# Sixteen full tiles of the expert lists worked beside the last group's scatters in a gated attention and mixture-of-experts block

## The chip, the core and the metric

The kernel runs on one core of a Trainium2 chip. The metric is the device time of one execution in microseconds (us), the median of several runs. The profile shows one further execution. Its span is the stretch from the first to the last instruction; what lies around the span is in the execution's own time.

## What is computed

The input is x of 16 x 128 x 256, a context tensor of the same shape, and weights. The reference, cut to what matters:

```python
# first half: x = x + tanh(g_xattn) * attention(ctx, ctx, layernorm(x))
kv_f = jnp.fft.rfft(einsum('bhil,bhjl->bijhl', k_, v_), n=2 * L)
y = jnp.fft.irfft(kv_f * kernel_f, n=2 * L)[..., :L]
out = einsum('bijhl,bhil->bjhl', y + kv * D, q_)
# second half: x = x + tanh(g_ffn) * ffn(layernorm(x)), for each of T = 2048 tokens
scores = sigmoid(xf @ w_router)                   # 32 experts
masked = where(best 4 of 8 groups, scores + corr_bias, -inf)
_, topk_idx = jax.lax.top_k(masked, 6)            # six experts for a token
eo = einsum('etm,emh->eth', silu(g) * u, down_w)  # 256 -> 176 -> 256 in each expert
routed = einsum('te,eth->th', combine, eo)
shared = silu(xf @ sh_gate_w) * (xf @ sh_up_w) @ sh_down_w
```

A token is one of 16 x 128 rows of 256 values. 2048 tokens with six experts each are 12288 rows of expert work.

## The kernel before

**Groups.** The sixteen batch rows go in four groups of GB = 4 (`group(g, ...)` on each engine; g runs from -1, which only makes the first attention, to 3, which only routes). In a group TensorE does the convolutions of the next group's attention, the router and the shared expert of this one; VectorE makes the attention sums and layernorms (L562 on), picks the experts (`choose`, L634) and finds each row's place in its expert's list (`place_rows`, L690). GpSimd (POOL) then writes the group's 4 x 128 tokens into the lists `expert_lists` in DRAM, with 24 indirect DMAs of 128 rows (L369). A row has 289 values: the normalised token, its number and its 32 scores. The rows wait in SBUF in one of two buffers `pay[g % 2]`; one lies in the arena, the other is `payload`.

**Weights.** The big SBUF region `arena` holds the attention's buffers first and the experts' weights `wgu` (gate and up) and `wd` (down, on 88 partitions) later. Thirteen experts' `wgu` is loaded early. The rest of `wgu` and the first 17 experts' `wd` are issued on ScalarE's DMA queue once the last attention is summed (L469, L471). `wd` of experts 17 to 24 lies over the scratch area and the arena's payload buffer, and is issued on ScalarE's queue after group 2's scatters and the tile tables (L500). `wd` of experts 25 to 31 is issued on SyncE's (SP's) queue after group 3's shared expert is added (L282).

**Tables.** After group 3's routing VectorE counts the rows of each expert (L783), cuts each list into tiles of 128 rows and makes a table with each tile's first row, expert and the rows that it has in common with the tile before (`describe_tiles`, `spread_tables`). PE spreads it over the partitions (L1021).

**Tiles.** Then all engines run through the tiles in blocks of four; 108 tiles run in this input. For tile t SP loads 128 rows of the list into `payload[:, t % 4]` (L289), PE transposes them (L1045), VectorE copies (L847), PE multiplies with `wgu` (L1054), ScalarE and VectorE make silu times up (L507, L865), PE transposes (L1064) and multiplies with `wd` (L1073), ScalarE scales by the token's score into a buffer (`copy_y`, L522; four buffers), and POOL adds the 128 rows to `token_sums` in DRAM with one indirect DMA (`add_tile`, L383), which waits for the add of three tiles before. SP's load of tile t waits until tile t - 3 has been picked from and transposed. Each engine works strictly in the order of its program; the semaphores named in the code are all that joins them.

**The turn from groups to tiles.** SP loads tile 0 only when `payload_free` has reached NG + 1, that is when all four groups' scatters have landed:

```python
            sp.wait_ge(payload_free, NG)
            sp.wait_ge(sh_added, GB)
            sp.dma_start(wd[:, WD_LAST * WD_E:E * WD_E], ...).then_inc(late_in, 16)
...
            sp.wait_ge(tables_ready, 1)
            sp.wait_ge(payload_free, NG + 1)
```

PE waits for all four weight transfers (`late_in` at 64) before its first tile. POOL issues group 3's scatters only after group 2's have landed, since it waits for a group's 24 before it goes on. At the end three partial sums are read back, added to x and stored.

## Time and profile before

| | us |
|---|---|
| median of 3 runs | 587.53 |
| lowest and highest | 586.39 and 587.93 |
| the profiled execution's own time | 592.33 |
| its span | 590.2 |
| TensorE busy in the span | 443.5 (75%) |
| VectorE, ScalarE, GpSimd busy | 313.5, 200.1, 301.0 |
| DMA traffic | 89.68 MB, mean 152 GB/s |

The profile has a page (busy times, the span in slices, the chain that ended last, the costliest groups of instructions) and views of single stretches: the chain of waits, the timeline, windows with each engine's busy time, and the DMA queues. Among the DMA queues q0 carries GpSimd's indirect transfers, q1 those that SP issues and q10 those that ScalarE issues. Times are counted from the start of the span.

### The profile page before, as it was taken

How to read it: one execution, taken by the hardware profiler on the slowest of the kernel's cores; microseconds unless marked ns; L12 is line 12 of the kernel's file. 1: busy time of each engine (PE TensorE's matmuls, PEld its weight loads, DVE VectorE, ACT ScalarE, POOL GpSimd, SP SyncE). 2: the span in 40 equal slices, each digit the busy share in tenths (PEclk: the TensorE clock that was granted, in tenths of full speed). 3: DMA queues.
4: the chain of work that ended last, by engine and by line, in shares of the span. 5: the costliest groups of instructions: out<-in, count | busy, mean ns of one | idle time of the engine just before them, and what ended most of it. 6: DMA issues, size and time to landing. Idle time of an engine off the chain costs nothing.

```text
span 590.2 us, 8581 instructions
## 1 busy us (share of the span) xinstructions
PE 443.5 (75%) x2098; PEld 334.7 (57%) x2098; DVE 313.5 (53%) x1141; ACT 200.1 (34%) x506; POOL 301.0 (51%) x240
## 2 busy tenths in 40 slices
PE   0181798789889666800599999999999999999700
PEld 0171676666767445500477777777777777777500
DVE  3679979966994804500344444444444444444227
ACT  2050633632553231100144444444444444444300
POOL 2800008865884760077066576666666666666610
PEclk9995889988969966955699999999999999999955
DMA  6999402221221498576356766666666666666488
GB/s 257 343 285 416 200 1 99 89 92 68 90 95 70 164 390 231 134 209 193 82 105 110 118 115 111 111 111 116 111 114 114 114 114 116 115 115 117 57 265 323
DMA packets 55706, 89.68 MB, mean 152 GB/s; under 512 B 6525, under 2 KB 49885, under 8 KB 55005
## 3 DMA queue, kind: packets, MB, share of 16 engines
q0 software_dynamic: 20160, 28.37, 28.4%
q1 hardware_dynamic: 35150, 49.33, 25.3%
q10 hardware_dynamic: 342, 11.35, 6.2%
q8 instruction: 23, 0.38, 0.3%
q14 instruction: 31, 0.25, 0.1%
HBM read 47.00 MB, written 42.03 MB: 151 GB/s over the span
## 4 chain that ended last, share of the span: by engine, by line
PE 67%; DVE 11%; issue 8%; DMA 5%; ACT 3%; POOL 2%; another core or an unknown queue 2%; SPq 1%; DVEq 0%; POOLq 0%; ACTq 0%
PE bank L1054 22%; PE bank L1073 15%; PE bank L943 6%; PE bank L914 4%; PE bank L1045 4%; PE bank L1064 4%; DVE arena L603 4%; PE bank L964 4%; PE bank L915 2%; DMA arena<-toeplitz 2%; PE bank L985 2%; DMA arena<-token_sums 2%; PE bank L934 2%; POOL work L354 1%
## 5 line engine op out<-in xcount | busy, mean ns | idle before, releaser
L383 POOL DMA_INDIRECT token_sums<-work,dest x108 | 168.3, 1558 | 113.8 <-ACT work L522 99.5
L1054 PE MATMUL bank<-wgu,work 128*128 x432 | 146.9, 463 | 0.0
L1073 PE MATMUL bank<-wd,work 88*128 x432 | 111.0, 379 | 0.0
L369 POOL DMA_INDIRECT expert_lists<-arena,slots x48 | 59.8, 1246 | 82.3 <-DVE slots L703 68.3
L865 DVE TENSOR_TENSOR work<-work,bank 128x176 f32<-128x176 f32 x108 | 36.4, 337 | 120.2 <-ACT work L507 120.2
L1054 PEld LDWEIGHTS bank<-wgu,work 128*128 128x128 f32 x432 | 74.1, 192 | 23.2 <-issue 0.5
L369 POOL DMA_INDIRECT expert_lists<-payload,slots x48 | 57.4, 1195 | 53.2 <-DMA expert_lists<-arena,slots 31.9
L507 ACT ACTIVATE work<-bank 128x176 f32<-128x176 f32 x108 | 34.2, 317 | 141.5 <-PE bank L1054 141.5
L847 DVE COPY work<-bank 128x256 f32<-128x256 f32 x108 | 45.8, 424 | 59.4 <-PE bank L1045 58.2
L1073 PEld LDWEIGHTS bank<-wd,work 88*128 88x128 f32 x432 | 73.3, 190 | 6.1 <-issue 0.2
L522 ACT ACTIVATE work<-bank,work 128x256 f32<-128x256 f32 x108 | 51.1, 473 | 53.6 <-issue 49.3
L1045 PE MATMUL bank<-ident,payload 128*128 128x128 f32 x216 | 42.2, 277 | 34.6 <-DMA payload<-expert_lists 34.6
L1045 PEld LDWEIGHTS bank<-ident,payload 128*128 128x128 f32 x216 | 30.8, 144 | 46.7 <-DMA payload<-expert_lists 35.8
L943 PE MATMUL bank<-shgu_sb,arena 128*128 128x352 f32 x128 | 49.1, 535 | 0.0
L914 PE MATMUL bank<-arena 128*128 128x288 f32 x128 | 44.0, 426 | 4.1 <-ACT arena L416 2.3
L603 DVE TENSOR_TENSOR arena<-arena,q_sb 128x448 f32<-128x448 f32 (+7 forms) x120 | 45.1, 451 | 2.2 <-ACT arena L416 2.2
L1064 PEld LDWEIGHTS bank<-ident,work 128*88 128x88 f32 x216 | 26.6, 123 | 29.9 <-issue 18.5
L1064 PE MATMUL bank<-ident,work 128*88 128x128 f32 x216 | 41.3, 273 | 0.0
L514 ACT COPY work<-bank 88x256 f32<-88x256 f32 x108 | 39.7, 367 | 0.0
L934 PE MATMUL bank<-ident,arena 128*128 128x128 f32 x48 | 9.8, 355 | 34.1 <-POOL arena L358 27.5
L943 PEld LDWEIGHTS bank<-shgu_sb,arena 128*128 128x128 f32 x128 | 27.7, 228 | 13.8 <-issue 6.2
L416 ACT COPY arena<-bank 128x288 f32<-128x288 f32 x64 | 25.3, 399 | 28.1 <-PE bank L915 27.0
(137 smaller groups left out, 506.8 us busy)
## 6 DMA issues: line engine op xcount, KB each, us to landing
payload<-expert_lists SPq DMA_DIRECT2D x108, 144.5 KB
wgu<-w_gu ACTq DMA_DIRECT2D x1, 6688.0 KB
arena<-token_sums SPq DMA_DIRECT2D x12, 512.0 KB, 8.3
expert_lists<-blank SPq DMA_DIRECT2D x1, 4768.5 KB, 26.7
wgu<-w_gu SPq DMA_DIRECT2D x1, 4576.0 KB, 17.5
token_sums<-blank SPq DMA_DIRECT2D x1, 4480.0 KB, 36.5
wd<-w_down ACTq DMA_DIRECT2D x1, 2992.0 KB
arena<-toeplitz SPq DMA_DIRECT2D x1, 2048.0 KB, 12.1
```

Source lines behind the costliest of these rows:

```text
L369: nc.gpsimd.indirect_dma_start(lists, bass.IndirectOffsetOnAxis(ap=slots[:, g % 2, b, k:k + 1], axis=0), pay[g % 2][:, b, :], None).then_i ...
L383: nc.gpsimd.indirect_dma_start(sums, bass.IndirectOffsetOnAxis(ap=dest[:, t % NPICK:t % NPICK + 1], axis=0), y_row(t), None, compute_op=AL ...
L514: nc.scalar.copy(win(work, HT_AT + t % 2 * L, [[1, L]], parts=MH), bank[4 + t % 2][0:MH, 0:L]).then_inc(t_hT_copied, 1)
L522: nc.scalar.activation(y_row(t), bank[6 + t % 2][:, 0:L], ACT.Identity, scale=pick_w(t)).then_inc(t_y_copied, 1)
L603: last = nc.vector.tensor_tensor(win(arena, Z_AT + z0, [[DH * DH, CELLS], [1, DH - d]]), y, win(q_sb, q_at + i0, [[DH, CELLS], [1, DH - d] ...
L847: nc.vector.tensor_copy(win(work, XT_AT + t % 2 * L, [[1, L]]), bank[t % 2][:, 0:L]).then_inc(t_x, 1)
L914: nc.tensor.matmul(y[:, 0:2 * CB], toe(h, 0), prods(s, hh, 0, 2), start=True, stop=False)
L943: last = nc.tensor.matmul(bank[5 + half][:, 0:SHM], x2T(b, k), shgu_sb[:, k, half * SHM:(half + 1) * SHM], start=(k == 0), stop=(k == KC - 1))
L1045: last = nc.tensor.transpose(bank[t % 2][:, k * P:(k + 1) * P], payload[:, t % NX, k * P:(k + 1) * P], ident[:, :])
L1054: last = nc.tensor.matmul(bank[2 + t % 2][:, 0:2 * M], xT_half(t, k), wgu[:, bass.ds(e * WGU_E + k * 2 * M, 2 * M)], start=(k == 0), stop= ...
L1064: last = nc.tensor.transpose(bank[4 + t % 2][0:MH, c * P:(c + 1) * P], win(work, H_AT + t % 2 * M + c * MH, [[1, MH]]), ident[:, :])
L1073: last = nc.tensor.matmul(bank[6 + t % 2][:, 0:L], hT_half(t, c), wd[:, bass.ds(e * WD_E + c * L, L)], start=(c == 0), stop=(c == 1))
```

## The change

Group 2's routing now also counts the rows that groups 0 to 2 have put in each list (twelve small matmuls and a copy to `count_a`). In group 3 VectorE makes a first table from it (`describe_known`), of the first NA = 16 tiles that are wholly filled, among the first 17 experts; PE spreads it and `spread_known` stores it. The later table leaves these tiles out (`taken_a`). SP loads tiles 0 to 3 when `payload_free` has reached NG (groups 0 to 2 have landed), then issues the last weights, then loads tiles 4 to 15, and only then waits for the second table and the last group's scatters. PE waits for two of the weight transfers before the first tile and for the other two at the gate matmuls of tile 16. Group payloads no longer lie in the arena, so the last two weight transfers are cut in another place: experts 17 to 21 on ScalarE's queue, 22 to 31 on SP's. Results wait in sixteen buffers, taken from arrays that are free by then, and `copy_y` of tile t waits for the add of tile t - 16.

The core of the diff:

```diff
-TMP_SIZE = 2912
+TMP_SIZE = 2432
...
-PAY_AT = TMP_AT + TMP_SIZE
-X2T_AT = PAY_AT + GB * ROW
+X2T_AT = TMP_AT + TMP_SIZE
...
-        pay = [win(arena, PAY_AT, [[ROW, GB], [1, ROW]]), payload[:, :, :]]
+        pay = [payload[:, :, :], payload_2[:, :, :]]
...
-            sp.wait_ge(payload_free, NG)
-            sp.wait_ge(sh_added, GB)
-            sp.dma_start(wd[:, WD_LAST * WD_E:E * WD_E], w_down[:, WD_LAST * WD_E:E * WD_E]).then_inc(late_in, 16)
-
...
+            sp.wait_ge(tables_a_ready, 1)
+            sp.wait_ge(payload_free, NG)
+            for t in range(NX):
+                load_tile(t)
+            sp.wait_ge(sh_added, GB)
+            sp.dma_start(wd[:, WD_LAST * WD_E:E * WD_E], w_down[:, WD_LAST * WD_E:E * WD_E]).then_inc(last_in, 16)
+            for t in range(NX, NA):
+                load_tile(t)
+
             sp.wait_ge(tables_ready, 1)
             sp.wait_ge(payload_free, NG + 1)
             last = last_block(sp)
-            for t in range(4 * (SURE + 1)):
+            for t in range(NA, 4 * (SURE + 1)):
                 load_tile(t)
...
             act.wait_ge(tables_ready, 1)
-            act.wait_ge(payload_free, NG)
             act.dma_start(wd[:, WD_MID * WD_E:WD_LAST * WD_E],
-                          w_down[:, WD_MID * WD_E:WD_LAST * WD_E]).then_inc(late_in, 16)
+                          w_down[:, WD_MID * WD_E:WD_LAST * WD_E]).then_inc(last_in, 16)
...
-                if t >= NX:
-                    act.wait_ge(t_added[t % NX], nth(t - NX))
+                if t >= YR:
+                    act.wait_ge(t_added[t % NX], nth(t - YR))
...
+                    if g == NG - 2:
+                        nc.vector.tensor_copy(count_a[:, :], bank[4][:, 2 * GB * E:(2 * GB + 1) * E])
...
+                    if not attend:
+                        describe_known(link)
...
+                    if not attend:
+                        spread_known()
+                    place_rows(*chosen)
...
+                chain(nc.vector.tensor_tensor(flat(nt, E), flat(nt, E), taken_a[:, :], ALU.subtract))
...
+                    else:
+                        pe.wait_ge(meta_a_ready, 1)
+                        for c in range(2):
+                            last = nc.tensor.matmul(bank[1][:, c * NA:(c + 1) * NA], win(arena, WIDE_A_AT + c * P, [[1, P]]),
+                                                    ident[:, 0:NA], start=True, stop=True)
+                        last.then_inc(meta_a_spread, 1)
...
+                    if g == NG - 2:
+
+                        for seen in range(KNOWN):
+                            last = nc.tensor.matmul(bank[4][:, 2 * GB * E:(2 * GB + 1) * E], ones_b[:, :],
+                                                    win(mask_b, seen * E, [[1, E]]), start=(seen == 0),
+                                                    stop=(seen == KNOWN - 1))
+                    last.then_inc(rank_ready, 1)
...
+                if t == NA:
+                    pe.wait_ge(last_in, 32)
...
-            pe.wait_ge(late_in, 64)
+            pe.wait_ge(late_in, 32)
```

SP's program at the turn from groups to tiles, before; `token_sums<-arena` are the stores of the shared expert of groups 0 to 2, `wd<-w_down` is L282:

```order
L272 DMA token_sums<-arena 128x256 [waits sh_stored,sh_copied] x11
L282 DMA wd<-w_down 88x3584 [waits sh_stored,sh_added,payload_free]
L200 TENSOR_LOAD tile_code [waits payload_free,tables_ready]
L200 ISA x2
L205 TENSOR_LOAD tile_row
L289 ISA
L289 DMA payload<-expert_lists 128x289
```

The same place now (from the last store on; tiles 1 and 2 left out); L312 is the same transfer with ten experts:

```order
L285 DMA token_sums<-arena 128x256 [waits sh_stored,sh_copied] x11
L216 TENSOR_LOAD tile_row [waits sh_stored,payload_free,tables_a_ready]
L298 ISA
L298 DMA payload<-expert_lists 128x289
...
L298 DMA payload<-expert_lists 128x289
L312 DMA wd<-w_down 88x5120 [waits sh_added]
L216 TENSOR_LOAD tile_row [waits t_xT,t_picked]
L298 ISA
L298 DMA payload<-expert_lists 128x289
```

Four tile loads have moved ahead of the weight transfer on SP's queue; twelve more stand behind it and ahead of the wait for the second table and the last scatters.

PE's program in group 2, from the transposes of the shared expert's first row to the next shared matmuls, before:

```order
L953 MATMUL bank<-ident,arena 88x128 x3
L998 MATMUL bank<-list_b,ones_b 128x128
L1000 MATMUL bank<-mask_b,ones_b 128x128 x8
L1003 MATMUL bank<-mask_b,ones_b 128x96 [waits mask_ready]
L1003 MATMUL bank<-mask_b,ones_b 128x64
L1003 MATMUL bank<-mask_b,ones_b 128x32
L1005 MATMUL bank<-mask_b,before_b 128x128
L943 MATMUL bank<-shgu_sb,arena 128x352 [waits sh_h_ready]
```

and now:

```order
L1034 MATMUL bank<-ident,arena 88x128 x3
L1085 MATMUL bank<-list_b,ones_b 128x128
L1087 MATMUL bank<-mask_b,ones_b 128x128 x8
L1090 MATMUL bank<-mask_b,ones_b 128x96 [waits mask_ready]
L1090 MATMUL bank<-mask_b,ones_b 128x64
L1090 MATMUL bank<-mask_b,ones_b 128x32
L1092 MATMUL bank<-mask_b,before_b 128x128
L1097 MATMUL bank<-mask_b,ones_b 128x32 x12
L1024 MATMUL bank<-shgu_sb,arena 128x352 [waits sh_h_ready]
```

The twelve counting matmuls stand between the rank matmuls, whose semaphore they now carry, and the shared expert.

## Rows read from the trace of the kernel before

**Rows 1.** The head of the page.
```profile
span 590.2 us, 8581 instructions
```

**Rows 2.** The chain of waits, 245 to 300: start us, us, what.
```profile
251.68 0.49 DVE rows L632
...
252.59 29.32 issue
...
284.65 2.27 DMA payload<-expert_lists
```

**Rows 3.** Timeline of POOL: start us, us, engine, line, operation [idle before <-releaser].
```profile
250.10 0.96 POOL L369 DMA_INDIRECT expert_lists<-payload,slots  x1 [31.86 <-DMA expert_lists<-arena,slots]
...
279.19 0.96 POOL L369 DMA_INDIRECT expert_lists<-payload,slots  x1 [0.30 <-issue]
```

**Rows 4.** Timeline of PE: transposes of tiles 0, 4 and 5.
```profile
285.98 0.69 PE L1045 MATMUL bank<-ident,payload 128*128 128x128 f32 x2 [34.34 <-DMA payload<-expert_lists]
...
294.21 0.38 PE L1045 MATMUL bank<-ident,payload 128*128 128x128 f32 x2
...
296.70 0.39 PE L1045 MATMUL bank<-ident,payload 128*128 128x128 f32 x2
```

**Rows 5.** Windows: stretch, length, PE PEld DVE ACT POOL, PEclk, DMA share, GB/s.
```profile
286.00:290.00 4.00, 3.70 (x9) 2.18 (x10) 1.23 (x5) 0.00 (x0) 0.00 (x0) 0.50 0.51 136
...
296.00:298.00 2.00, 2.00 (x10) 1.46 (x10) 1.14 (x5) 0.87 (x3) 1.34 (x1) 1.00 0.31 70
...
320.00:400.00 80.00, 80.00 (x387) 59.28 (x386) 36.64 (x160) 33.97 (x96) 50.67 (x33) 1.00 0.68 113
```

**Rows 6.** Timeline: issue of the last two weight transfers.
```profile
249.33 0.30 ACTq L500 DMA_DIRECT2D wd<-w_down  x1
...
252.25 0.34 SPq L282 DMA_DIRECT2D wd<-w_down  x1
```

**Rows 7.** DMA queues in 250 to 258.5: packets, MB, share of 16 engines.
```profile
q10 hardware_dynamic: 77, 1.26, 66.1%
q0 software_dynamic: 98, 0.31, 10.7%
q1 hardware_dynamic: 1, 0.01, 0.5%
```

**Rows 8.** DMA queues in 258.5 to 269.
```profile
q1 hardware_dynamic: 98, 1.25, 39.0%
q0 software_dynamic: 349, 1.09, 33.3%
q10 hardware_dynamic: 22, 0.18, 5.9%
```

**Rows 9.** DMA queues in 269 to 276, the only queue that is active.
```profile
q0 software_dynamic: 496, 1.55, 71.9%
```

**Rows 10.** Timeline: VectorE's rank wait in group 2, then group 3.
```profile
184.24 0.29 DVE L697 SCALAR_TENSOR_TENSOR arena<-bank,mask_b 128x128 f32<-128x128 f32 x1 [6.06 <-PE bank L1005]
...
219.85 0.28 ACT L478 ACTIVATE payload<-bank 128x128 f32<-128x128 f32 x1 [9.30 <-remote]
...
220.16 0.17 DVE L638 COPY payload<-tok_id 128x4 f32<-128x4 f32 x1 [15.14 <-ACT payload L478]
...
228.82 0.63 PE L1010 MATMUL bank<-mask_b,ones_b 128*128 128x32 bf16 x16
229.14 0.29 DVE L697 SCALAR_TENSOR_TENSOR arena<-bank,mask_b 128x128 f32<-128x128 f32 x1 [2.90 <-PE bank L1005]
...
239.19 0.19 DVE L798 TENSOR_TENSOR arena<-arena 128x32 f32<-128x32 f32 x1
```

**Rows 11.** Timeline of POOL in the tiles: adds, two of them back to back.
```profile
319.28 1.57 POOL L383 DMA_INDIRECT token_sums<-work,dest  x1 [2.11 <-issue]
321.15 1.57 POOL L383 DMA_INDIRECT token_sums<-work,dest  x1 [0.30 <-issue]
...
560.64 1.56 POOL L383 DMA_INDIRECT token_sums<-work,dest  x1 [0.30 <-issue]
```

More of the change, by code:

```diff
@@ L62 @@
 assert WD_AT <= TMP_AT
-WORK = 3072
+WORK = 2048
 NX = 4
-NPICK = 8
+NPICK = 24
+YR = 16
 XT_AT = 0
@@ L757, in group, with describe_known, tmp, flat @@
                 return count[0]
+            def describe_known(link):
+                at = [KNOWN_AT]
+                def tmp(n):
+                    at[0] += n
+                    return at[0] - n
+                def flat(o, n=1):
+                    return win(arena, o, [[1, n]])
+                PAD, FULL = E // 2, KNOWN * HD // P
+                cmp = tmp(EA * FULL)
+                run = [tmp(PAD + E), tmp(PAD + E)]
+                upto = tmp(1 + E)
+                past, pn, ex, first, off, high, meta = tmp(E), tmp(E), tmp(1), tmp(1), tmp(1), tmp(1), tmp(2)
+                assert at[0] <= WIDE_A_AT
+                nc.vector.memset(flat(run[0], PAD + E), 0.0)
+                nc.vector.memset(flat(run[1], PAD), 0.0)
+                nc.vector.memset(flat(upto), 0.0)
+                link(nc.vector.tensor_tensor(win(arena, cmp, [[FULL, EA], [1, FULL]]), win(count_a, 0, [[1, EA], [0, FULL]]),
+                                             win(tile_at, 1, [[0, EA], [1, FULL]]), ALU.is_ge))
+                link(nc.vector.tensor_reduce(flat(run[0] + PAD, EA), win(arena, cmp, [[FULL, EA], [1, FULL]]), AX, ALU.add))
+                nc.vector.tensor_copy(taken_a[:, :], flat(run[0] + PAD, E))
+                s, src = 1, 0
+                while s < E:
+                    link(nc.vector.tensor_tensor(flat(run[1 - src] + PAD, E), flat(run[src] + PAD, E),
+                                                 flat(run[src] + PAD - s, E), ALU.add))
+                    s, src = 2 * s, 1 - src
+                last = run[src] + PAD
+                link(nc.vector.tensor_scalar(flat(past, E), flat(last, E), lane[:, 0:1], None, ALU.is_le))
+                nc.vector.tensor_scalar(flat(upto + 1, E), flat(last, E), float(NA), None, ALU.min)
+                link(nc.vector.tensor_tensor(flat(pn, E), flat(past, E), taken_a[:, :], ALU.mult))
+                nc.vector.tensor_tensor(taken_a[:, :], flat(upto + 1, E), flat(upto, E), ALU.subtract)
+                nc.vector.tensor_reduce(flat(ex), flat(past, E), AX, ALU.add)
+                link(nc.vector.tensor_reduce(flat(first), flat(pn, E), AX, ALU.add))
+                nc.vector.tensor_scalar(flat(meta + 1), flat(ex), float(EA - 1), None, ALU.min)
+                nc.vector.tensor_scalar(flat(high), flat(ex), -float(LIST), float(E * LIST), ALU.mult, ALU.add)
+                link(nc.vector.tensor_scalar(flat(off), lane[:, :], flat(first), float(P), ALU.subtract, ALU.mult))
+                link(nc.vector.tensor_tensor(flat(off), flat(off), flat(high), ALU.min))
+                link(nc.vector.scalar_tensor_tensor(flat(meta), flat(ex), float(LIST), flat(off), ALU.mult, ALU.add))
+                nc.vector.tensor_copy(win(arena, WIDE_A_AT, [[P, 2], [1, P]]),
+                                      win(arena, meta, [[1, 2], [0, P]])).then_inc(meta_a_ready, 1)
@@ L792, in describe_tiles @@
                     s, src = 2 * s, 1 - src
-                nc.vector.tensor_scalar(tile_code[:, NT:NT + 1], flat(run[src] + PAD + E - 1), -1.0 - 4 * SURE, None, ALU.add)
-                past, pn, full, ex, first, n_e, last_e = (
-                    tmp(E), tmp(E), tmp(E), tmp(1), tmp(1), tmp(1), tmp(1))
+                nc.vector.tensor_scalar(tile_code[:, NTILES:NTILES + 1], flat(run[src] + PAD + E - 1), -float(BEYOND), None,
+                                        ALU.add)
+                past, pn, full, ex, first, n_e, last_e, skip, a_e = (
+                    tmp(E), tmp(E), tmp(E), tmp(1), tmp(1), tmp(1), tmp(1), tmp(E), tmp(1))
                 chain(nc.vector.tensor_scalar(flat(full, E), flat(nt, E), 0.0, None, ALU.is_gt))
@@ L1004, in group @@
                                          start=False, stop=False)
[L1005 to L1006 removed]
+                    last = nc.tensor.matmul(rank(0), before_b[:, :], win(mask_b, g * GB * E, [[1, GB * E]]),
+                                            start=False, stop=True)
+                    if g == NG - 2:
[4 more added lines that the diff above has]
+                    last.then_inc(rank_ready, 1)
                     if not attend:
```

67 lines of the change are left out of this document (44 added, 23 removed).

## Prediction

> **What bounds the kernel now.** I read the page first, then the chain of waits between the groups and the tiles, then the timelines of POOL and PE there, and last the DMA queues. The tile loop is TensorE's: in 320 to 400 PE is busy for all of the 80 us at the full clock [rows 5], and the transposes of tiles 4 and 5 stand at 294.21 and 296.70, so a tile costs 2.49 us [rows 4]. 108 of them are 269 us of a span of 590.2 [rows 1]. Nothing in the change makes a tile cheaper. What it can take is the gap ahead of them. VectorE ends the group work at 251.68 + 0.49 = 252.2, and then the chain shows 29.32 us in which it finds nothing to name [rows 2]; PE stood idle for 34.34 us when tile 0's transpose started at 285.98 [rows 4]. The timeline of POOL fills that hole: it had waited 31.86 us for group 2's scatters to land, issued group 3's first at 250.10 and the last of 24 at 279.19, so 23 steps of 1.265 us [rows 3]. POOL's issue rate sets this stretch, and SP holds the tile loads until it is over.
>
> **What the change asks for.** Groups 0 to 2 have landed at about 249.9, just ahead of POOL's 250.10 [rows 3]. The new SP program can read the first table and issue load 0 at about 250.6 (I allow 0.7 us for what SP does before a load). Alone a load lands 2.27 us after its issue [rows 2]. Sixteen full tiles do exist: counted from the reference's routing, groups 0 to 2 fill 39 blocks of 128 rows in the lists of the first 17 experts, and the table takes nine of expert 0 and seven of expert 1. The others are 91, rounded to 92 by the blocks of four, so 108 tiles run as before and the loop's own length does not change. All that moves is the moment at which PE reaches its steady step. I take tile 4's transpose as the mark, 294.21 before, because from there on each tile follows after 2.49 us.
>
> **Added ahead of it, on the path.** In group 2 twelve counting matmuls precede the rank semaphore; VectorE waits for that (6.06 us idle until PE L1005) [rows 10]. Sixteen such matmuls took 0.63 us in group 3 [rows 10], so twelve are 0.47; the copy of the count before the places may add 0.1. In `describe_tiles` one chained step like L798, 0.19 us [rows 10], precedes the shared expert's next multiply. Together 0.8 us; bounds 0.2 (all in waits) and 1.5. **Added at no cost:** `describe_known` is about 23 short VectorE operations, some 5 us, put where VectorE idled 15.14 us until ScalarE's L478 [rows 10]; without that cover it would cost the 5 us. `spread_known`, four short operations, falls into the 2.90 us in which VectorE waits for group 3's ranks [rows 10]. The other new steps of `describe_tiles` end before PE asks for the table. ScalarE's weight issue loses the wait for group 2, which was over at about the same time, and gains nothing.
>
> **Where the first tiles meet the last weights.** This is the term that decides. Before, the last two weight transfers were issued at 249.33 (ScalarE's queue, q10) and 252.25 (SP's queue, q1) [rows 6]. The queue view shows how slowly they went: until 258.5 q10 moved 77 packets and q1 one [rows 7]; q1's 1.25 MB went in 258.5 to 269 [rows 8]; from 269 only POOL's q0 was active [rows 9]. So the second transfer began to move only when the first was nearly through, some 6 us after its issue, and both together held the queues from about 251 to 269. The change cuts the same 15 experts' `wd` as 5 and 10 rather than 8 and 7: the same bytes, so I keep the 18 us. On SP's queue they now stand between load 3 and load 4, as the program order shows. Loads 0 to 3 come first, and each takes some of the DMA engines' time: in 296 to 298 the loads alone held a share of 0.31 [rows 5], which at one load per 2.49 us is 0.77 us a load, 3.1 us for four. If a load cannot pass an earlier transfer of its own queue, load 4 lands at 269 + 0.8 + 3.1 + 0.8 (its own) = 273.7. The bounds: 269 if the first loads slip into idle time, 277 if the larger pieces go slower.
>
> The Trainium skill bears on this. DMA: Bandwidth & Descriptors, section Queues, rings and completion order, states that each DMA engine takes a queue's descriptors in ring order; by that rule load 4 waits for the weights, which no row here shows, since no load stood behind a large transfer before. The same section states that an engine goes round-robin between the queues it has work for. By that q1 would have taken turns with q10 from about 254; the trace does not agree, with one packet of q1 up to 258.5 [rows 7]. Under it loads 0 to 3 would land near 253 rather than 259, but load 4 would not move, and the sum would be the same.
>
> **Tiles 0 to 3 and the restart.** Loads 0 to 3 land by about 259, behind the first transfer. From tile 0's transpose to tile 4's took 294.21 - 285.98 = 8.2 us [rows 4], so PE would reach tile 4 at about 267 and wait some 6 us for load 4. PE's clock was at the lower of its two levels (0.50) in 286 to 290, after PE had been idle, and full in 296 to 298 [rows 5]. I expect the same 4 us at half speed after the second pause: 2.0 us of work lost; bounds 0 (the clock holds) and 2.0.
>
> **Behind it.** The loads of tiles 5 to 15 are issued three tiles ahead, beside scatters whose queue held a share of 0.72 in 269 to 276 [rows 9]. With 0.31 for the loads that is just full, so they may come late for a few us until POOL's scatters end near 282; I take 0, bounds 0 and 3. Tile 16 needs the second table, the last scatters (landed by about 283) and the last weights (273); it comes at 273.7 + 2 + 12 x 2.49 = 305.6, so none of them is late. POOL starts the adds at about 283.5 with some eight results waiting. Back to back they went at 321.15 - 319.28 = 1.87 us [rows 11] against 2.49 for a tile, so POOL has caught up within some 30 adds. Sixteen buffers cover the wait. The end stays as it is.
>
> **The sum.** 294.21 - 273.7 - 2.0 = 18.5 us earlier. Against the profiled execution, 592.33 - 18.5 = 573.8. The median lies 4.8 us under that execution, and I keep this distance: 587.53 - 18.5 = 569.0. The likeliest case's own range, from the bounds, is 563 to 573.
>
> **Rivals.**
> 1. *The loads are not held behind the weights* (or these go faster): tiles run on from load 0, which lands between 253 and 259. Against 285.98, with the 0.8 us, the gain is 26 to 32 us: 555.5 to 561.5. For it: DMA engines that carry no piece of an 88-partition transfer stay free, and q1 as a whole moved only 39% [rows 8]. Against it: a load is complete only when its slowest part is. Chance 0.2.
> 2. *The stretch loses more*: either loads 5 to 8 starve beside the scatters, or an engine stalls in group 3 as ScalarE did while the weights streamed (9.30 us until L478, released by nothing that the profile can name) [rows 10]; the code grew on PE and VectorE there. 4 to 10 us less gain: 573 to 579. Chance 0.17.
> 3. *The first tiles wait for the last scatters after all*: POOL's queue would have to be served ahead of the loads until 282. The packets of q0 and of the weights moved side by side [rows 8], which speaks against it. 587.5 and a little. Chance 0.04.
> 4. *Slower: the adds become the bound.* They now start at 283.5 with a backlog. If an add takes more than (560.64 - 283.5) / 107 = 2.59 us, the last one [rows 11] ends later than before, whatever PE does; at 2.75 it would be 17 us later, 604. The waits for the add three before, with tile loads beside them, could do this; the 1.87 us measured back to back says no. Chance 0.04.
>
> **How the numbers follow.** The likeliest case has 0.55. With its range, most of rival 1 and the near part of rival 2, 557 to 575 should hold the time 8 times in 10. Faster than before by over 0.3% (1.8 us, about what a measurement of this kernel can tell from no change) are the likeliest case and rivals 1 and 2: 0.92. Within 0.3%: 0.04. Slower: 0.04.
>
> **What would show it.** In the new profile: loads 0 to 3 issued at 250 to 253 and tile 0's transpose by 259; PE idle for some 6 us before tile 4, released by the payload DMA; q1's weights moving up to about 273; tile transposes 2.49 us apart from there; POOL's scatters still at 1.265 us each until about 280; adds from 283.5 at 1.87 us until they meet ScalarE's pace. It would be wrong if PE runs through tiles 3 and 4 without a pause (rival 1), if it pauses again after tile 5 (rival 2), or if POOL waits for its own adds and never catches up (rival 4).

## The result

| | before | changed |
|---|---|---|
| median of 4 runs | 586.96 (585.89 to 587.93) | 578.06 (576.73 to 580.32) |
| profiled execution, its span | 592.33, 590.2 | 577.85, 576.0 |

The change took 8.9 us off: a ratio of 0.9846, interval 0.9824 to 0.9868. I had forecast 18.5 us (569.0, range 557 to 575), so the direction was right and the size was not. The time lies in rival 2's 573 to 579, but partly by luck: the loads of tiles 5 to 8 did not starve, and ScalarE's wait in group 3 was in both kernels already.

The experiments below ran on six chips (e1 to e4, e5 and e6, h1 to h4, e7 with i1, j1 to j3, k1 to k3), and they show that this one number is half of the story. On four of them the kernel before takes 582.2 to 584.1 us, and on the three of these where the changed kernel ran beside it the change brings 15.6 to 16.0 us. On the other two, and where this result was taken, before takes 587 to 591. I call the first kind quiet chips and the second kind stalling chips, for what their traces show: in all nine profiles of the second kind ScalarE waits 9.3 to 12.0 us at one place in group 3, and in the eleven of the first kind it waits nowhere over 5 us there. One of the three executions of the kernel before that stand beside j1 to j3 was in a slower state (603.17) and is left out of their ratios.

**The profile after (a stalling chip).** GpSimd's (POOL's) timeline; these rows answer [rows 3]:

```profile
245.58 0.96 POOL L387 DMA_INDIRECT expert_lists<-payload,slots  x1 [30.43 <-DMA expert_lists<-payload,slots]
...
274.63 0.96 POOL L387 DMA_INDIRECT expert_lists<-payload,slots  x1 [0.30 <-issue]
280.88 1.61 POOL L401 DMA_INDIRECT token_sums<-y_rows,dest  x1 [5.29 <-ACT y_rows L539]
...
305.00 1.57 POOL L401 DMA_INDIRECT token_sums<-shgu_sb,dest  x1 [2.12 <-issue]
306.88 1.57 POOL L401 DMA_INDIRECT token_sums<-shgu_sb,dest  x1 [0.30 <-issue]
```

The scatters (GpSimd's indirect writes of rows into the lists) keep their 1.26 us. They start 4.5 us earlier than in [rows 3]; but those of groups 1 and 2, which the change hardly touches, also start 1.8 and 4.3 us earlier (135.68 and 181.72 against 137.49 and 186.06). That one profiled execution before was late by itself, so part of the difference of the spans is not the change's. The adds start when ScalarE delivers and never fall behind.

PE's timeline, against [rows 4]: tiles 0 to 3, tile 4 (271.71), tile 5 (281.68), tile 6 (284.91).

```profile
253.88 0.69 PE L1140 MATMUL bank<-ident,payload 128*128 128x128 f32 x2 [4.20 <-DMA payload<-expert_lists]
256.04 0.69 PE L1140 MATMUL bank<-ident,payload 128*128 128x128 f32 x2 [1.47 <-issue]
...
258.87 0.59 PE L1140 MATMUL bank<-ident,payload 128*128 128x128 f32 x2
...
260.69 0.38 PE L1140 MATMUL bank<-ident,payload 128*128 128x128 f32 x2
260.91 1.35 PE L1151 MATMUL bank<-wgu,work 128*128 x4
...
271.71 0.69 PE L1140 MATMUL bank<-ident,payload 128*128 128x128 f32 x2 [5.50 <-issue]
...
281.68 0.63 PE L1140 MATMUL bank<-ident,payload 128*128 128x128 f32 x2
...
284.91 0.39 PE L1140 MATMUL bank<-ident,payload 128*128 128x128 f32 x2
```

Tile 4's transpose comes at 271.71, where I had 273.7. That is closer than it should be, since the scatters started 4.5 us earlier: counted from the first scatter it is 26.1 us and I had 23.6. Its idle time is put down to "issue", not to its load, but q1, the queue of the last weights and the loads, tells which it was. In 266 to 270, 270 to 274 and 274 to 278 it moved (packets, MB, share of 16 engines):

```profile
q1 hardware_dynamic: 101, 0.31, 29.5%
q1 hardware_dynamic: 216, 0.22, 16.8%
q1 hardware_dynamic: 2, 0.00, 0.0%
```

A load alone is 144 packets. From 268, when the weights were nearly through, to 274 q1 moved some 304, which is loads 4 and 5 one after the other; so by this count (an estimate) load 4 landed at about 271, just ahead of the transpose, and load 5 before 274. Yet tile 5's transpose comes at 281.68, ten us after tile 4's rather than 4.5. ScalarE's timeline tells more; its first row answers L478 in [rows 10]:

```profile
218.09 0.28 ACT L496 ACTIVATE payload<-bank 128x128 f32<-128x128 f32 x1 [11.90 <-remote]
...
264.58 0.37 ACT L531 COPY work<-bank 88x256 f32<-88x256 f32 x1 [3.23 <-remote]
277.88 0.32 ACT L524 ACTIVATE work<-bank 128x176 f32<-128x176 f32 x1 [12.93 <-remote]
```

ScalarE waits until 277.88 for the gate product of tile 2, which PE has in the records at 260.91 to 262.26. "Remote" means that no record of this core fits the release. ScalarE went on some 15 us after the recorded end, 3 us after the last scatter was issued. The ends of matmuls are modelled, so whether the product, its signal or ScalarE itself was late can't be read. Below I call this a late signal.

### The profile page after: what moved, and what is told of

It reads as the page before. It is cut to its first block, busy times and chain, and to the rows that moved or that the text cites. A ratio compares the mean times of both kernels' runs of the same rounds, so it can differ in the third digit from the quotient of the medians.

```text
span 576.0 us, 8645 instructions
## 1 busy us (share of the span) xinstructions
PE 450.1 (78%) x2114; PEld 337.8 (59%) x2114; DVE 319.0 (55%) x1173; ACT 200.0 (35%) x506; POOL 298.1 (52%) x240
## 4 chain that ended last, share of the span: by engine, by line
PE 61%; DMA 12%; DVE 9%; POOL 6%; issue 4%; ACT 3%; another core or an unknown queue 3%; SPq 1%; DVEq 0%; POOLq 0%; ACTq 0%
PE bank L1151 22%; PE bank L1170 16%; DMA expert_lists<-payload,slots 5%; PE bank L995 5%; POOL expert_lists L387 4%; PE bank L1140 4%; PE bank L1024 4%; PE bank L1161 4%; DVE arena L620 3%; PE bank L996 2%; DMA arena<-toeplitz 2%; PE bank L1066 2%; DMA arena<-token_sums 2%; DMA payload<-expert_lists 1%
## 5 line engine op out<-in xcount | busy, mean ns | idle before, releaser
L387 POOL DMA_INDIRECT expert_lists<-payload,slots x96 | 116.5, 1214 | 134.1 <-DVE slots L723 75.7
L1151 PE MATMUL bank<-wgu,work 128*128 x432 | 148.5, 467 | 0.0
L1170 PE MATMUL bank<-wd,work 88*128 x432 | 112.2, 382 | 3.1 <-issue 2.6
L401 POOL DMA_INDIRECT token_sums<-q_sb,dest x28 | 43.6, 1558 | 26.1 <-ACT q_sb L539 23.3
L401 POOL DMA_INDIRECT token_sums<-shgu_sb,dest x28 | 43.6, 1558 | 24.7 <-ACT shgu_sb L539 19.6
L401 POOL DMA_INDIRECT token_sums<-shd_sb,dest x24 | 37.4, 1557 | 22.4 <-ACT shd_sb L539 14.9
L995 PE MATMUL bank<-arena 128*128 128x288 f32 x128 | 45.2, 437 | 3.1 <-ACT arena L434 1.8
L401 POOL DMA_INDIRECT token_sums<-y_rows,dest x21 | 32.8, 1561 | 24.9 <-ACT y_rows L539 21.8
## 6 DMA issues: line engine op xcount, KB each, us to landing
wgu<-w_gu SPq DMA_DIRECT2D x1, 4576.0 KB, 18.5
arena<-toeplitz SPq DMA_DIRECT2D x1, 2048.0 KB, 11.8
```

Source lines behind the costliest of these rows:

```text
L387: nc.gpsimd.indirect_dma_start(lists, bass.IndirectOffsetOnAxis(ap=slots[:, g % 2, b, k:k + 1], axis=0), pay[g % 2][:, b, :], None).then_i ...
L401: nc.gpsimd.indirect_dma_start(sums, bass.IndirectOffsetOnAxis(ap=dest[:, t % NPICK:t % NPICK + 1], axis=0), y_row(t), None, compute_op=AL ...
L995: nc.tensor.matmul(y[:, 0:2 * CB], toe(h, 0), prods(s, hh, 0, 2), start=True, stop=False)
L1151: last = nc.tensor.matmul(bank[2 + t % 2][:, 0:2 * M], xT_half(t, k), wgu[:, bass.ds(e * WGU_E + k * 2 * M, 2 * M)], start=(k == 0), stop= ...
L1170: last = nc.tensor.matmul(bank[6 + t % 2][:, 0:L], hT_half(t, c), wd[:, bass.ds(e * WD_E + c * L, L)], start=(c == 0), stop=(c == 1))
```

## What held the tiles back on a stalling chip: four experiments

My theory A was that the last weights, on the same queues, hold everything in 250 to 270. All four ran on one stalling chip (before: 591.03, 13 runs); the changed kernel itself did not run there, so I compare ratios.

**e1: no last weights.**

```diff
-            sp.dma_start(wd[:, WD_LAST * WD_E:E * WD_E], ...).then_inc(last_in, 16)
...
-            act.dma_start(wd[:, WD_MID * WD_E:WD_LAST * WD_E], ...).then_inc(last_in, 16)
...
-                    pe.wait_ge(last_in, 32)
```

> Leaves out the down weights of experts 17 to 31: the last two weight transfers are not made, and the tiles use no expert above 16 for their weights (same work, other numbers). Theory A (the last weights hold up the first tiles twice: loads 4 on stand behind them in SP's queue, and PE's results of tile 2 come some 15 us late while they stream): both go, tile 4's transpose about 10 us after tile 0's, no wait of 8 us or more on ScalarE or VectorE between 250 and 285, and the time falls by 8 to 14 us against the changed kernel, to 564 to 570. Theory B (the engines stall on something else of the first tiles, such as code or the scatters): the stall near 262 to 278 stays, and the gain is under 4 us.

578.97, ratio 0.9817 (0.9762 to 0.9873), an interval that takes in the change's own 0.9846: no gain that can be told from the changed kernel. PE's timeline, tiles 4, 5 and 6:

```profile
262.50 0.38 PE L1136 MATMUL bank<-ident,payload 128*128 128x128 f32 x2
282.35 0.63 PE L1136 MATMUL bank<-ident,payload 128*128 128x128 f32 x2
286.00 0.38 PE L1136 MATMUL bank<-ident,payload 128*128 128x128 f32 x2
```

Tile 4 is 9 us earlier and tile 5 stays at 282. ScalarE's wait for tile 2's product is still there (275.07, 13.67 us). Theory A falls for this chip.

**e2: both transfers on ScalarE's queue. e3: one transfer for each of the fifteen experts.**

```diff
+            act.dma_start(wd[:, WD_LAST * WD_E:E * WD_E], ...)      # e2; removed on SP's queue
...
+            for e in range(WD_LAST, E):                             # e3; the same on ScalarE's
+                sp.dma_start(wd[:, e * WD_E:(e + 1) * WD_E], ...)
```

> The ten experts' down weights are issued on ScalarE's queue, behind the five of before it, instead of SP's. Theory A1 (the order in SP's queue is what costs): load 4 lands by 262, tiles go on, and the time falls by 6 to 10 us. Theory A2 (PE's results come late whenever weights stream, whichever queue): tile 4's load lands early, but ScalarE still waits some 13 us for tile 2's gate product, and the time changes by less than 3 us.

> The last two weight transfers are cut into one DMA per expert (5 on ScalarE's queue, 10 on SP's), 2 KB a partition each; same bytes, same order. If large pieces are what holds the engines up, the 13 us wait of ScalarE near 265 to 278 shrinks to under 4 us and the time falls by 4 to 8 us, though load 4 still lands near 271. If it is the bytes or the queue order, within 2 us of the changed kernel.

579.88 (0.9824, 0.9773 to 0.9876) and 580.03 (0.9825, 0.9771 to 0.9879); tile 5's transpose at 282.0 and 283.7. Queue and size of the pieces don't matter for the time here, since tile 5 waits for something else. For tile 4 they do, and I had not expected it of e3: its transpose came at 269.40 in e2 and at 264.48 in e3, against 271.71 in the changed kernel. In pieces the weights were through sooner: from 246 to 262 q1 moved 2.4 MB in e3 and 1.5 in the changed kernel. What e3's pieces alone are worth on a quiet chip was not tried.

**e4: all that the change adds, but tile 0 waits for the last scatters.**

```diff
             sp.wait_ge(payload_free, NG)
-            for t in range(NX):
-                load_tile(t)
             sp.wait_ge(sh_added, GB)
             sp.dma_start(wd[:, WD_LAST * WD_E:E * WD_E], ...)
+            sp.wait_ge(payload_free, NG + 1)
+            for t in range(NX):
+                load_tile(t)
```

> All of the change but its purpose: SP waits for the last group's scatters before tile 0's load, as the kernel before does. Both theories: the price of the added counting, table and waits alone. By the prediction's 0.8 us it stands within 0 to 2 us above the kernel before, 587 to 589; if the additions cost more, or the new places of buffers cost or gain, it shows here.

588.75, ratio 0.9969 (0.9939 to 0.9999), a little below the kernel before and not above it. Taken together the first table, the counting matmuls and the new buffers cost nothing that can be measured; whether one of them costs what another gains was not split. Its tiles start at 284.00 and then run undisturbed, though ScalarE waited 10.67 us in group 3: among the tiles, the stall comes only where they meet scatters.

## Are the scatters the cause? And the chip?

Theory S: the scatters, while GpSimd issues them, hold the other engines' signals back. Theory C: it is the first pass through the tile loop's instructions that stalls, wherever it comes. Later theory D: whether there is a stall at all depends on the chip.

**e5 and e6: hold back half or all of the last group's scatters until eight tiles are done.**

```diff
                 for b in range(GB):
+                    if g == NG - 1 and b == GB // 2:                # e5; e6: the same wait ahead of all 24
+                        pool.wait_ge(t_y_copied, 8)
```

> GpSimd holds the last group's 24 scatters back until ScalarE has copied the results of eight tiles; all else is as in the changed kernel, and nothing is left out. The three runs so far show the 13 to 14 us stall of tiles 2 to 4 ending when the scatters end (about 275 to 278), with and without the last weights. Theory S (scatters being issued are what holds PE's results and the engines' steps back): with GpSimd quiet until then, tiles 0 to 7 run with no stall; the transpose of tile 5 comes at 262 to 272 (281.68 in the changed kernel), as the last weights' transfers allow, then a tile each 2.5 us, ScalarE copies tile 7 at 276 to 282, the scatters run from there for 30 us, and a stall of about ten us or more appears in tiles 8 to 15 instead, during them. Total 578 to 592. Theory C (it is the first passage through the tile loop's instructions, whose fetch comes late, which stalls): the stall stays at tiles 2 to 4, the transpose of tile 5 at 278 to 284, the scatters begin at 290 or later, and the total is 592 to 605. If neither, theory W: only scatters and traffic together: no stall at all, total as in S without its second stall, 575 to 583.

> Twelve of the last group's 24 scatters are issued at once (about 245.6 to 260.8), the other twelve when ScalarE has copied the results of eight tiles; nothing is left out. Theory S: the stall of tiles 2 to 4 ends when the first twelve end, about 262 to 264 and not 275 to 278, so it is at most 3 us long; the transpose of tile 5 at 265 to 273; the second twelve start at 280 to 284 and end at 296 to 299, and a second stall stands in tiles 8 to 15. Total 570 to 580. Theory C: the stall keeps its 13 us and tile 5's transpose stands at 278 to 284; total 582 to 590, since the second twelve start only after tile 7 (290).

e6 took 590.52 and e5 578.02, beside a before of 584.13. In both, tile 5's transpose came at 271.2 or 271.3 and nothing stalled. The times are what they are because tile 16 waits for the scatters held back; in e6 it comes at 322.42. But e6's scatters, from 287 on, ran beside tiles 12 to 15 without any stall either, which theory S had not allowed, and ScalarE's 9 to 12 us wait in group 3 was gone, where nothing had been changed. That led to theory D, the chip.

**h1 to h4: the changed kernel, the kernel before, e5 and e1 again, on one other chip.**

> The changed kernel as it is, on the same chip as the three runs beside it. In the two runs with scatters held back no engine waited on a late semaphore, neither in tiles 2 to 4 nor in group 3, where nothing had been changed; there ScalarE had waited 9 to 12 us in every earlier profile. So either the stall depends on the program (theory S, as before: scatters with tile work) or on the chip or the execution (theory D). Theory S: the stall is back in both places here; tile 5's transpose at 280 to 284, 0.982 to 0.987 of before. Theory D, if this chip is one without the stall: tile 5's transpose at 268 to 274, no wait of ScalarE over 6 us in group 3, and the time is 568 to 573, which is what I forecast for the change; if it is one with the stall, all four runs have it.

> The kernel before as it is. Theory D: where the stall is absent ScalarE's 9.30 us wait in group 3 is absent too, but the last group's scatters start at the same 245 to 250 us, since they wait for the landing of group 2's scatters and not for ScalarE; so 582 to 588 without the stall and 586 to 592 with it. Theory S: the 9 us wait is there on any chip.

> The kernel with twelve of the last scatters at once and twelve after eight tiles, again. Theory S: no late semaphore in either place, 577 to 579, tile 5's transpose at 271. Theory D on a chip with the stall: ScalarE waits 9 us or more in group 3 and again in tiles 2 to 4, until the first twelve scatters end or a little longer, and the time is 580 to 588.

> The last two weight transfers left out and the tiles' experts clamped to the first sixteen, again. Without the stall (theory D on such a chip) nothing holds load 4: tile 4's transpose at 258 to 262, tile 15's at 286 to 290, and the last tile's transposes wait for the last group's scatters at tile 16 instead (not before 277): 562 to 568. With the stall as in its first run: tile 5's transpose at 282, 577 to 581.

Theory D's forecast came, with a time a little under its 568 to 573. The changed kernel took 566.72 against 582.70: 16.0 us less, ratio 0.9728 (0.9698 to 0.9758). Again beside later experiments, on two more quiet chips, it had 0.9751 (0.9724 to 0.9777; i1) and 0.9714 (0.9678 to 0.9750; k3). The kernel before in h2 took 583.49; its last scatters started at 240.07 and not at the 245 to 250 that I had expected. PE's timeline of h1, tiles 0 to 6:

```profile
246.19 0.69 PE L1140 MATMUL bank<-ident,payload 128*128 128x128 f32 x2 [15.14 <-DMA payload<-expert_lists]
247.65 0.69 PE L1140 MATMUL bank<-ident,payload 128*128 128x128 f32 x2 [0.78 <-DMA payload<-expert_lists]
250.48 0.63 PE L1140 MATMUL bank<-ident,payload 128*128 128x128 f32 x2
252.44 0.38 PE L1140 MATMUL bank<-ident,payload 128*128 128x128 f32 x2
264.44 0.69 PE L1140 MATMUL bank<-ident,payload 128*128 128x128 f32 x2 [9.35 <-DMA payload<-expert_lists]
268.82 0.38 PE L1140 MATMUL bank<-ident,payload 128*128 128x128 f32 x2
271.31 0.38 PE L1140 MATMUL bank<-ident,payload 128*128 128x128 f32 x2
```

and of h2, tiles 4 and 5:

```profile
283.53 0.38 PE L1045 MATMUL bank<-ident,payload 128*128 128x128 f32 x2
286.02 0.38 PE L1045 MATMUL bank<-ident,payload 128*128 128x128 f32 x2
```

This is the forecast's picture: tiles 0 to 3, a pause that the payload DMA ends, and 2.49 us a tile from tile 5 on, beside scatters that run until 273.23. The line of the page with the chain by engine parts the two kinds of chip in all profiles but one: "another core or an unknown queue" has 2 or 3% on stalling chips (j2 below has none) and nothing on quiet ones. The changed kernel on a stalling chip, then h1:

```profile
PE 61%; DMA 12%; DVE 9%; POOL 6%; issue 4%; ACT 3%; another core or an unknown queue 3%; SPq 1%; DVEq 0%; POOLq 0%; ACTq 0%
```
```profile
PE 63%; DMA 15%; DVE 9%; POOL 6%; ACT 3%; issue 3%; SPq 1%; POOLq 0%; ACTq 0%; DVEq 0%
```

h3 took 576.17 (0.9886): tile 16 waits for the second twelve scatters and comes at 306.08, against 296.22 in h1. h4 took 550.69 (0.9453), 16.0 us under h1, and 11 us or more below the 562 to 568 that I had expected: I had allowed for loads that starve beside the scatters, and they don't. PE's timeline, tile 4:

```profile
252.27 0.38 PE L1136 MATMUL bank<-ident,payload 128*128 128x128 f32 x2
```

264.44 - 252.27 = 12.2 us: on a quiet chip theory A is right, and the last weights are what holds load 4. Not all of it is the wait behind them. The last scatters also start 3.7 us earlier in h4 (240.45 against 244.14), since no weights move beside the landing of group 2's.

**j1 and j2: e5 and e6 once more.** This chip was a stalling one (before: 588.65).

> Twelve of the last scatters at once, twelve after eight tiles. If before is at 586 or more here (a chip with the stall): theory S says that the late semaphores of tiles 2 to 4 end with the first twelve scatters, so tile 5's transpose at 268 to 276 and 577 to 583; theory C says that they last 13 us wherever the scatters are, tile 5's at 280 or later, 584 to 592. If before is at 581 to 585: as twice already, tile 5's at 271, 576 to 578.

> All 24 of the last scatters after eight tiles. Before at 586 or more: theory S says no late semaphore in tiles 0 to 7, tile 5's transpose at 269 to 274 and late semaphores in tiles 11 to 15 during the scatters; theory C says the 13 us stay at tiles 2 to 4, tile 5's at 280 or later. Before at 581 to 585: as in its first run, tile 5's at 271 and 588 to 592.

580.49 and 595.94 (ratios 0.9868, interval 0.9777 to 0.9960, and 1.0131, 1.0043 to 1.0218; two runs each). Tile 5's place in both (274.84 and 271.50) and j1's time came as theory S had them. PE's timeline of j2, tiles 4, 5, then 13, 14, 15:

```profile
266.54 0.69 PE L1142 MATMUL bank<-ident,payload 128*128 128x128 f32 x2 [5.00 <-DMA payload<-expert_lists]
271.50 0.42 PE L1142 MATMUL bank<-ident,payload 128*128 128x128 f32 x2
...
291.46 0.38 PE L1142 MATMUL bank<-ident,payload 128*128 128x128 f32 x2
293.95 0.39 PE L1142 MATMUL bank<-ident,payload 128*128 128x128 f32 x2
298.91 0.64 PE L1142 MATMUL bank<-ident,payload 128*128 128x128 f32 x2
```

ScalarE's in the same run, group 3 and then tiles 13 to 15, while the scatters run from 287.43 to 316.52:

```profile
217.76 0.28 ACT L498 ACTIVATE payload<-bank 128x128 f32<-128x128 f32 x1 [10.65 <-remote]
...
301.75 0.47 ACT L541 ACTIVATE shgu_sb<-bank,work 128x256 f32<-128x256 f32 x1 [3.95 <-remote]
310.93 0.32 ACT L526 ACTIVATE work<-bank 128x176 f32<-128x176 f32 x1 [8.71 <-remote]
315.14 0.37 ACT L533 COPY work<-bank 88x256 f32<-88x256 f32 x1 [3.89 <-issue]
321.53 0.47 ACT L541 ACTIVATE shgu_sb<-bank,work 128x256 f32<-128x256 f32 x1 [6.03 <-remote]
```

With no scatters tiles 4 to 11 run free, on a chip where group 3 stalled for 10.65 us. With the scatters the late signals are back, at other tiles and other instructions. So the stall follows the scatters and not the place in the program, and it needs the chip: theory S and theory D are each half of it. These are single profiles, but e7's kernel on this same chip (j3, below) has its scatters early again and stalls between tiles 4 and 6 again. It does not start with the first scatter: in j2 some six pass before tile steps lengthen, and in j1 the first twelve (246.76 to 260.67) leave tile 5 at 274.84.

One rival was not tested by an edit: that an engine's next code comes late beside the scatters. The profile shows the loads of code as two more DMA queues, q8 and q14 ("instruction"), and j2 speaks against this rival. From 288 to 332, where the waits above stand, only two queues moved anything:

```profile
q0 software_dynamic: 1867, 4.21, 35.1%
q1 hardware_dynamic: 1008, 1.04, 9.8%
```

e6, the same kernel on a quiet chip, has the same gap in its code loads and no wait. So no code that landed there ended those waits. For the waits of tiles 2 to 5 in the changed kernel, where one load of code moved at 266 and others at 269 and 281, the trace doesn't settle it.

## A version that is faster on quiet chips, and two open terms

**e7: the last weights one expert at a time between the loads.**

```diff
             for t in range(NX, NA):
                 load_tile(t)
+                for e in range(WD_MID, E):
+                    if (e - WD_MID) * (NA - NX) // (E - WD_MID) == t - NX:
+                        sp.dma_start(wd[:, e * WD_E:(e + 1) * WD_E], ...).then_inc(last_in, 16)
```

Nothing goes out on ScalarE's queue.

> The down weights of the last fifteen experts go out one expert at a time on SyncE's queue, one or two behind each of the loads of tiles 4 to 15, and nothing on ScalarE's queue; nothing is left out. Where engines don't stall (kernel before at 581 to 585), leaving these weights out took 16.0 us off the changed kernel (566.72 to 550.69), since load 4 no longer lay behind them. If it is the place in the ring that costs this, tile 4's transpose comes at 250 to 257 (264.44 in the changed kernel), tile 15's at 280 to 290 and the total is 550 to 558. If it is the traffic itself (2.6 MB beside scatters and loads), tile 4's is early but the tiles run at 3 to 4 us each while the weights move, tile 16's transpose comes near 296 and the total is 563 to 567. On a chip with the stall (before at 586 to 592) PE's results come late until the scatters end whatever the order: tile 5's at 278 or later, 572 to 578.

> The changed kernel as it is, beside the interleaved one, and a third sample of theory D: the before kernel's time tells which kind of chip this is. Before at 581 to 585: no wait of ScalarE over 6 us in group 3, tile 5's transpose at 268 to 273, the change worth 14 to 18 us. Before at 586 to 592: ScalarE waits 9 us or more in group 3, tile 5's transpose at 280 or later, the change worth 7 to 11 us.

> The last weights one expert at a time between the loads. Before at 586 or more: late semaphores until the scatters end, tile 5's transpose at 276 to 284, 572 to 578. Before at 581 to 585: 550 to 552.5 as in its first run.

On a quiet chip 551.02 against 582.76, ratio 0.9468 (0.9443 to 0.9492), with the changed kernel at 567.14 beside it. The weights are all there and it is as fast as h4 without them. PE's timeline, tiles 4 and 5:

```profile
252.33 0.38 PE L1140 MATMUL bank<-ident,payload 128*128 128x128 f32 x2
254.82 0.38 PE L1140 MATMUL bank<-ident,payload 128*128 128x128 f32 x2
```

So the same bytes need not cost the 16 us. They have two parts. Counted from the first scatter, tile 5 comes at 13.7 us in e7 and at 25.5 in i1: 11.8 us are the place of the weights, and their pieces, in SP's queue, with the restart that falls away. The other 4.3 are the scatters' earlier start (241.08 against 245.35), now that nothing goes out on ScalarE's queue beside group 2's landing; k1 below has the same 4.5 us from that alone. Place and pieces were not parted on a quiet chip. On the stalling chip of j1 it took 577.29 (0.9814, 0.9772 to 0.9856), about what the change gained at its own measurement (0.9846), and 26 us more than on the quiet chip: tile 4 at 256.74, tile 5 at 276.03, with ScalarE waiting 13.25 us in between.

**k1: ScalarE's wait for group 2 put back. k2: e7 with at most six scatters under way.**

```diff
             act.wait_ge(tables_ready, 1)
+            act.wait_ge(payload_free, NG)                           # k1
...
                 for b in range(GB):
+                    if g == NG - 1 and b > 0:                       # k2
+                        pool.wait_ge(scattered, (g * GB + b) * TOPK * 16)
```

> The changed kernel with the removed wait put back: ScalarE's queue sends the middle weights only when group 2's scatters have landed. On a chip without the stall the weights then no longer run beside the landing of those scatters, so the last group's scatters start at 239 to 242 (244.14 and 245.35 without the wait) and tile 0's transpose comes at 241 to 244. If the landing of the last weights follows the start of this stretch, tile 4's comes 3 to 4 us earlier too (260 to 262) and the total is 562 to 564. If it follows from the bytes, which now start 12 us later, tile 4's stays at 263 to 267 and the total is within 2 us of the changed kernel beside it. On a chip with the stall ScalarE sends them at 245 in either case: no difference over 2 us.

> The interleaved kernel, and GpSimd waits after each six of the last group's scatters until they have landed, so that at most six are under way. Without the stall: scatters end 5 to 8 us later (275 to 280), tile 16 isn't touched by that, 550 to 554. With the stall: if it comes from many scatters under way, ScalarE's longest wait in tiles 2 to 5 is under 5 us, tile 5's transpose at 256 to 262 and the total is 556 to 566; if from scatters as such, the stall lasts until they end, 276 to 284, and the total is 577 to 584.

> The changed kernel as it is. Before at 581 to 585: 565 to 568. Before at 586 to 592: 576 to 580.

A quiet chip. k1 took 567.73 against k3's 566.24; the intervals of their ratios overlap (0.9715 to 0.9798, 0.9678 to 0.9750). Its scatters started at 241.09 and not at 245.62, but tile 4 came at 268.14 and not at 266.34: the bytes decide, as the second branch of the expectation said, though 268.14 is 1 us beyond its 263 to 267. Tile 0 came at 249.53, not at 241 to 244: loads 0 to 3 now went out just behind ScalarE's transfer (issued at 240.31) and not 15 us after it. k2 took 558.93, over the 550 to 554 that I had expected and 8 us more than e7 on its own quiet chip: after each of the first three sixes GpSimd stood idle for 3.3 to 4.8 us until they had landed, the last scatter started at 283.03 and tile 16 came at 289.47, 8.0 us after tile 15. Whether few scatters under way cure the stall stays open, since k2 met no stalling chip.

## Why the prediction was wrong, and where it was right

| after the last group's first scatter, us | before | changed |
|---|---|---|
| stalling: that scatter, tile 4, tile 5 | 250.10, 44.1, 46.6 | 245.58, 26.1, 36.1 |
| quiet (h2, h1): the same | 240.07, 43.5, 45.95 | 244.14, 20.3, 24.7 |

- **What bounds the kernel: right.** The loop stayed at 2.49 us a tile; what moved is the gap before it (from tile 5 to the end of the span the changed kernel took 294.3 us and the kernel before 293.5).
- **The step that failed is "they may come late for a few us ...; I take 0, bounds 0 and 3".** That term was a delay of tiles 5 to 15 beside the scatters. On the measured chip the stretch from the first scatter to tile 5 shrank by 10.5 us (46.6 - 36.1) and not by 18.5. Of the 8.0 us that are missing 5.5 lie between tiles 4 and 5 (10.0 us for 4.5), where ScalarE had to wait 12.93 us for PE's product while scatters ran; the other 2.5 lie before tile 4. Of the 9.6 us by which the medians miss the forecast this is the greater part; 0.8 lie behind tile 5 and the rest wasn't found. It was not the loads that starved: load 5 had landed before 274. The sign stood in [rows 10]: 9.30 us of ScalarE's, released by nothing that the profile can name, while group 2's scatters were being issued. I used it only for rival 2, at 0.17. Before, a disturbance at the turn cost nothing, because PE had no tile to work on; the change moved work into it. Why signals are late beside scatters on some chips stays open.
- **Additions, 0.8 us: right or less.** In e4 all of the change but its purpose took 0.3% off (0.9939 to 0.9999).
- **Load 4 behind the weights: right in place and nearly in size, where nothing else is late.** I had tile 4 move by 20.5 us; from h2 to h1 it moved by 283.53 - 264.44 = 19.1. That the two are so close is in part luck: h1's scatters start 4.1 us later than h2's (see ScalarE's weight issue below), and from the first scatter tile 4 stands at 20.3 us, where I had 23.6. h4 and e7 show that the weights ahead of load 4 do it. The Trainium skill, DMA: Bandwidth & Descriptors, section Queues, rings and completion order, has descriptors consumed in ring order on each engine; by that rule the trace agrees: counted from the first scatter, tile 4 comes at 21.0 us in i1, behind the weights, and at 11.3 in e7, with one expert's weights or two ahead of each load. On the stalling chip the term was hidden: without the weights (e1) tile 5 stayed at 282. The price of a load in that sum, 0.77 us, was misread: the share of 0.31 in 296 to 298 [rows 5] is not the loads alone but 0.219 of q1 and 0.095 of an add on q0, so a load is 0.55 us and load 4's landing would have been 272.5.
- **That the two weight queues don't take turns: not so in general.** I read it from one packet of q1 beside 77 of q10 [rows 7]. In the changed kernel, in 246 to 250, loads of q1 moved beside ScalarE's weights with about as many packets, though with a ninth of the bytes:

```profile
q10 hardware_dynamic: 66, 0.68, 70.2%
q1 hardware_dynamic: 72, 0.08, 9.4%
```

- **Restart at half clock, 2.0 us: right.** In h1 tile 5 follows tile 4 after 4.38 us, 1.9 more than the 2.49. The windows of h1 (columns as in [rows 5]) have the clock at 0.50, its lower level, after the pause:

```profile
264.00:268.00 4.00, 3.56 (x9) 2.42 (x10) 0.56 (x2) 0.38 (x2) 2.95 (x4) 0.50 0.67 239
271.00:275.00 4.00, 4.00 (x21) 2.94 (x20) 2.07 (x10) 1.55 (x5) 2.58 (x3) 1.00 0.51 169
```

- **"ScalarE's weight issue loses the wait ..., and gains nothing": wrong in its reason.** On a quiet chip the issue moves from 239 to 228, beside group 2's landing scatters, and these land some 4 us later (the last group's first scatter at 244.14 against 240.07 in h2, and 245.62 in k3 against 241.09 in k1); the weights being gone earlier gives back about as much (k1).
- **Rival 1** (not held behind the weights) was wrong as a forecast, but its 555.5 to 561.5 became possible on a quiet chip once the order was changed (e7, 551.02). **Rival 4** did not come: adds ran at 1.88 us back to back and caught up.

## What to carry to other kernels

A wait that nothing in the profile explains is a cost that can follow the work: before moving an engine's work into such a stretch, price the stretch at what its unexplained waits show, not at zero. Put a large transfer that is needed late behind small loads that are needed now, in pieces, on the same queue; here that was worth 16 us where nothing stalls, and nothing that can be told where it does. And when a result misses, measure the same two kernels on another chip before looking for the cause in the code.

## What the runs showed of the hardware

- The same program differs by chip: the kernel before at 582.2 to 584.1 us on four, 587.0 to 591.0 on two and in the result; the changed kernel at 566 to 567 on three quiet ones, 578 in the result. The overlap makes the difference larger: from 3 to 9 us before to some 11 us. Whether it is the chip, the core used on it, or where its memory lies was not told apart.
- On stalling chips engines go on with PE's results up to 15 us after their recorded ends while GpSimd's indirect writes run, and in the tile loop only then; the traffic of the weights is neither needed (e1) nor enough (j2 before 287). What inside the chip holds them was not found.
- On quiet chips 24 indirect writes, 12 tile loads and 2.6 MB of weights run beside a tile loop at its full pace (e7).
- A batch of six indirect writes lands 4 to 6 us after the last one's start (k2, 4.3 to 5.8), so pacing them by landings costs 8 us here.
